# Causal triangle of a score maximum added in 64-row tiles instead of 128-row tiles

## The reference

```python
q = (x @ Wq + bq).reshape(b, t, 16, 8).transpose(0, 2, 1, 3)     # 16 heads of 8
k = ...; v = ...                                                # 4 groups, each repeated for 4 heads
q, k = _rope(q), _rope(k)
scores = jnp.einsum('bhtd,bhsd->bhts', q, k) / sqrt(8)
scores = jnp.where(tril, scores, -inf)
probs = jax.nn.softmax(scores, axis=-1)
attn = jnp.einsum('bhts,bhsd->bhtd', probs, v)
out = attn.transpose(0, 2, 1, 3).reshape(b, t, 128) @ Wo + bo
```

## Time and profile before

| what | us |
|---|---|
| median of 3 runs | 2346.62 (2346.45 to 2359.24) |
| span of the profiled execution | 2345.2 |
| PE busy | 2106.0 (90%) |
| DVE busy | 1792.4 (76%) |
| ACT busy | 1629.6 (69%) |
| POOL busy | 1377.0 (59%) |
| L648 in the causal stage, PE busy: pa, pc, pb | 50.3, 36.7, 31.1 (256, 256 and 192 products) |

### The profile page before, as it was taken

One profiled execution on the slowest core, in us unless ns is written; L12 is line 12 of the kernel. 1 busy time (PEld: TensorE's weight loads), 2 busy tenths in 40 slices (PEclk: granted clock), 3 DMA queues, 4 the chain that ended last, 5 costly groups with the idle time before them and its releaser, 6 DMA issues. The chain is left out here.

```text
span 2345.2 us, 55664 instructions
## 1 busy us (share of the span) xinstructions
PE 2106.0 (90%) x19389; PEld 1356.7 (58%) x19516; DVE 1792.4 (76%) x3455; ACT 1629.6 (69%) x3312; POOL 1377.0 (59%) x2085
## 2 busy tenths in 40 slices
PE   2999999999999368999999999999999999999971
PEld 1555555555555246666666666666666666666641
DVE  2788787787877266888888888886888788787736
ACT  1676576666767346888878878776877787777745
POOL 3587687777876675465564655554564564564403
PEclk8999999999999668999999999999999999999985
DMA  1000001000100101101001010111011001001014
GB/s 35 2 20 24 16 15 29 15 15 15 29 15 10 37 17 47 32 18 33 16 16 32 16 32 16 27 34 31 18 26 26 18 21 31 18 17 34 18 33 112
DMA packets 50491, 59.34 MB, mean 25 GB/s; under 512 B 8144, under 2 KB 43392, under 8 KB 48256
## 3 DMA queue, kind: packets, MB, share of 16 engines
q1 hardware_dynamic: 50304, 56.58, 9.7%
HBM read 17.90 MB, written 8.39 MB: 11 GB/s over the span
## 5 line engine op out<-in xcount | busy, mean ns | idle before, releaser
L974 POOL TENSOR_TENSOR b_part_b<-b_raw,b_tabs 128x256 f32<-128x256 f32 x512 | 431.8, 873 | 326.5 <-ACT b_raw L1033 291.8
L983 POOL TENSOR_TENSOR b_qk<-b_qk,b_part_b 128x1024 f32<-128x1024 f32 x128 | 332.4, 2597 | 282.5 <-DVE b_qk L1133 275.3
L1133 DVE TENSOR_TENSOR b_qk<-b_raw,b_tabs 128x512 f32<-128x512 f32 x256 | 282.2, 1141 | 0.1
L417 POOL TENSOR_TENSOR a_idle<-a_idle 128x1 f32<-128x1 f32 x432 | 83.3, 193 | 232.2 <-ACT a_probs L511 163.4
L1234 PE MATMUL b_work<-b_w_high,b_h_high 128*128 128x512 f32 x384 | 190.6, 496 | 29.6 <-DVE b_h_low L1123 19.0
L468 POOL TENSOR_SCALAR_AFFINE_SELECT a_probs<-a_probs 128x256 f32<-128x256 f32 x512 | 204.5, 411 | 0.0
L579 DVE TENSOR_REDUCE a_qpack<-a_pc 128x2 f32<-128x768 f32 (+1 forms) x128 | 139.4, 1089 | 61.6 <-PE a_pc L648 60.0
L1261 PE MATMUL b_work<-ident,b_qk 128*128 128x128 f32 x1024 | 161.3, 289 | 25.9 <-issue 15.7
L1305 PEld LDWEIGHTS b_work<-b_v_even,b_pT 128*64 128x64 f32 x2048 | 138.5, 139 | 78.4 <-issue 75.8
L679 PE MATMUL a_work<-a_probs,a_v 128*32 128x512 f32 (+3 forms) x2048 | 182.8, 453 | 1.1 <-POOL a_probs L468 0.8
L1060 ACT COPY b_pT<-b_work 128x512 f32<-128x512 f32 x256 | 155.5, 608 | 35.9 <-PE b_work L1295 35.8
(11 more groups left out here) (206 smaller groups left out, 5481.1 us busy)
## 6 DMA issues: line engine op xcount, KB each, us to landing
b_v_even<-b_v SPq DMA_DIRECT2D x32, 528.0 KB, 4.4
b_v_even<-b_v SPq DMA_DIRECT2D x32, 396.0 KB, 5.8
a_x_in<-in_L_attn_x SPq DMA_DIRECT2D x16, 256.0 KB, 3.2
a_x_again<-in_L_attn_x SPq DMA_DIRECT2D x16, 256.0 KB, 3.3
x_scratch<-a_x SPq DMA_DIRECT2D x16, 256.0 KB, 2.4
out<-c_y SPq DMA_DIRECT2D x4, 1024.0 KB, 5.4
b_w_raw<-in_L_ffn_wqkv SPq DMA_DIRECT2D x2, 768.0 KB, 4.4
b_tabs<-tab SPq DMA_DIRECT2D x2, 512.0 KB, 4.1
```

Of the source, the lines that this page charges most:

```text
L974: last = pool.tensor_tensor(part_b[:, x, :].rearrange("p (h d) -> p h d", d=DH)[:, :, lo:lo + DH // 2], raw[:, i % 2, x, :].rearrange("p ( ...
L983: pool.tensor_tensor(qk[:, i], qk[:, i], part_b[:], ALU.add).then_inc(c_made, 1)
L1133: last = dve.tensor_tensor(qk[:, i, x, :].rearrange("p (h d) -> p h d", d=DH), raw[:, i % 2, x, :].rearrange("p (h d) -> p h d", d=DH), ta ...
```

## The change

The triangle is added by four products of 64 rows instead of two of 128. The first two (a = 0 and 1) add it to the queries 0 to 63 of a block over all 128 keys, the other two to the queries 64 to 127 over the keys 64 to 127; nothing is masked for those below. The stationary operand is a slice of `half_of`, ones on a diagonal of a 64 x 192 field, once in each half of the partitions: by its start column (64 or 0) the ones stand in the columns of the first or the second half of the queries. The moving operand is `mask_half`, the triangle for 64 queries, also held twice. The setup makes them with one more memset, and three more selects.

```diff
--- before.py
+++ after.py
@@ -304,7 +304,8 @@
         bo_b = sb("bo", [P, D])
         cos = sb("cos", [P, TT, QK1])
         sin = sb("sin", [P, TT, QK1])
-        mask_ts = sb("mask_ts", [P, P], BF16)
+        mask_half = sb("mask_half", [P, P], BF16)
+        half_of = sb("half_of", [P, P + HALF], BF16)
 
         xn = sb("xn", [P, TT, D])
         xT = sb("xT", [D, T])
@@ -343,7 +344,7 @@
         freed = {name: sem(f"a_{name}_freed") for name in bank_of}
         flow = Banks(PLAN1, bank_of, filled, freed)
 
-        LOADS, CONSTS_MADE = 16, 12
+        LOADS, CONSTS_MADE = 16, 16
         transfers = lambda b, slot: (b - slot) * 8
         halves = lambda a: slice(HALF * a, HALF * a + HALF)
 
@@ -398,14 +399,21 @@
 
         @block.gpsimd
         def _(pool):
-            for t, val in [(ident, 0.0), (ident_bf, 0.0), (mask_ts, 0.0), (qpack, 0.0), (kpack, 0.0), (v, 1.0), (idle, 0.0)]:
+            for t, val in [(ident, 0.0), (ident_bf, 0.0), (mask_half, 0.0), (half_of, 0.0), (qpack, 0.0), (kpack, 0.0), (v, 1.0),
+                           (idle, 0.0)]:
                 pool.memset(t[:], val).then_inc(consts_made, 1)
-            pool.wait_ge(consts_made, 7)
+            pool.wait_ge(consts_made, 8)
             for t in (ident, ident_bf):
                 pool.affine_select(out=t[:], in_=t[:], compare_op=ALU.not_equal, fill=1.0, base=0,
                                    pattern=[[-1, P]], channel_multiplier=1).then_inc(consts_made, 1)
-            pool.affine_select(out=mask_ts[:], in_=mask_ts[:], compare_op=ALU.is_ge, fill=MASKED, base=0,
-                               pattern=[[-1, P]], channel_multiplier=1).then_inc(consts_made, 1)
+            for a in range(2):
+                r = slice(HALF * a, HALF * a + HALF)
+                pool.wait_ge(consts_made, 10 + 2 * a)
+                pool.affine_select(out=mask_half[r, :], in_=mask_half[r, :], compare_op=ALU.is_ge, fill=MASKED, base=0,
+                                   pattern=[[-1, P]], channel_multiplier=1).then_inc(consts_made, 1)
+                pool.affine_select(out=half_of[r, :], in_=half_of[r, :], compare_op=ALU.not_equal, fill=1.0, base=HALF,
+                                   pattern=[[-1, P + HALF]], channel_multiplier=1).then_inc(consts_made, 1)
+            pool.wait_ge(consts_made, 14)
             for e in range(2):
                 pool.memset(packed_k(e, NEG_MAX, 1), 1.0).then_inc(consts_made, 1)
             pool.wait_ge(consts_loaded, 16 * LOADS)
@@ -644,10 +652,13 @@
                         r = halves(a)
                         pe.matmul(x[:, a, n * w:(n + 1) * w], qT[r, slot, j, i * P:(i + 1) * P], kT[r, slot, gp, 0:w],
                                   start=(n == 0), stop=False, skip_group_check=True)
-                for a in range(2):
-                    last = pe.matmul(x[:, a, 0:len(js) * w].rearrange("p (j s) -> p j s", s=w)[:, :, i * P:w], ident_bf[:],
-                                     mask_ts[:].rearrange("p (a c) -> p a c", a=1).to_broadcast([P, len(js), P]),
-                                     start=False, stop=True, skip_group_check=True)
+                for first in (0, HALF):
+                    for a in range(2):
+                        r, n = halves(a), P - first
+                        last = pe.matmul(x[:, a, 0:len(js) * w].rearrange("p (j s) -> p j s", s=w)[:, :, i * P + first:w],
+                                         half_of[r, HALF - first:HALF - first + P],
+                                         mask_half[r, 0:n].rearrange("p (a c) -> p a c", a=1).to_broadcast([HALF, len(js), n]),
+                                         start=False, stop=True, skip_group_check=True)
                 last.then_inc(full, 1)
 
             def max_turn(l, b, j, slot):
```

## The result

The kernel after takes 2329.41 us (2324.02 to 2330.76, 4 runs), the kernel before 2347.36 beside it (2346.45 to 2359.24): a ratio of 0.9908, interval 0.9885 to 0.9931. The forecast was 2326. Its sum was not right in its parts, though: in the profiled execution, which took 2324.02 us, the causal stage gave 31 us where 21 were expected, and the stage behind it, whose code is unchanged, took 7 back.

What follows compares the result with a forecast made beforehand. PE was taken to lead 15 of a causal step's 44 us, DVE and POOL the other 29. 14 x 1.13 + 5 x 0.9 + 0.7 = 21 us off the median 2346.6 gave 2326 us, range 2304 to 2342.

Steps and rivals of the forecast that it cites:

- The prices of the fills: Mask cost per score-bank fill: one head saves 0.14 or 0.27 or loses 0.02, four heads save 0.43; 3.8 us a step.
- loads in front: Rival, chance 0.05: mask products wait for weight loads not fetched ahead behind f32 tiles, 1.6 us a step more, 2370.
- loads eat it: Rival, chance 0.14: each fill's four mask loads are not covered and use up the shape-change savings; 6 us left, 2340.
- issue: Rival, chance 0.03: issuing small products costs 0.054 each, so four masks take 0.22, 0.13 more than priced; 2344.
- PE bounds all: Rival, chance 0.06: PE bounds the whole causal step, so all 3.8 us count in 15 steps, 57 us; 2289.
- The slack is larger than I read: Rival, chance 0.22: DVE and POOL stretches hide waits or some fills move them forward; half the sum counts, 37 us, 2308.
- so PE has 0.11 to spare there: At values 9, behind POOL's apply and selects: PE starts 0.16 after them, a real wait takes 0.05; 0.11 us gained.
- Fills 13 to 10: Score-bank fills 13, 6, 3, 2, 7, 11, 16, 10, in the stretch from values 9 that PE was said to lead.
- the loss at fill 2: Its bank is read until 419.07, so of 0.61 us that PE would be earlier, 0.36 turns into waiting.
- fill 14: One-head masks before a 64*128 group, in the stretch that PE leads: saves 0.27 us.
- 0.12 to spare: DVE's cast starts 0.16 after POOL's rotary chain ends, so PE's earlier finish gains 0.12 us there.
- The steps with a jump: Five causal steps where the hardware loop jumps back and PE stands 2.83 us: more fills count, 0.9 us extra each.

Runs made afterwards that it cites:

- e_shape: The changed kernel with each of its four 64-row mask products over all 128 keys, the tile shape without the saved columns: 2327.72 us, ratio 0.9921 to before.

## Why the forecast came out near, and what failed in it

**The prices of the fills held.** No 0.11 stands in front of the masks, the next 64*128 group pays one load, transposes pay the change of shape. The loads of the four products are hidden. By lines, their group over the causal stage:

```profile
L658 PEld LDWEIGHTS a_pc<-a_mask_half,a_half_of 64*128 64x128 bf16 x512 | 15.0, 96 | 20.0 <-issue 15.2
```

96 ns each, beside 97 for 128 rows and 187 for the f32 ones; since four masks with their loads pass in 0.09 us before a 64*128 group, they cannot lie in front of the products or be bound by issue. That ends three rivals (loads in front, loads eat it, issue). The Trainium skill (TensorE: Matmul & The Clock Gate, "Weight-path perf modes — Fast Weight Load (FWL) and DoubleRow") says that the quick load is on for 128 weights of a type that is not FP32. The two lengths agree with it and halving the rows does not undo it; no run here switches it off for a bf16 load. The Trainium skill (TensorEngine Tiling (Array Packing), "Key Properties") says that a change of tiling mode drains TensorE. The trace fits it: the masks' start came 0.10 nearer to the scores', and e_shape shows that the shape, not the columns, is most of the gain. No run tells a drain from the weight loading that the prediction took those 0.11 us for.

**The rivals on the slack.** "PE bounds all" fell with PE's idle time of 1.34 us. "The slack is larger than I read" came closest for the causal stage: 31 us, between the forecast's 21 and its 37 (which make 2310, not the 2308 that stands beside them).

**The step that failed** is the second of the chain, "so PE has 0.11 to spare there", at *values* 9. *Values* 9 stands behind that select in the list, but the count it waits for belongs to an earlier one, which had ended some 2 us before. What closes the stretch over DVE and POOL is u_turn, 4.3 us earlier (410.85), and its spare was 0.59. The step in three parts, from starts in the rows:

| part of the step | before | after | saved | predicted |
|---|---|---|---|---|
| x_turn to POOL's first rstd (398.12 - 381.64; 384.33 - 368.02) | 16.48 | 16.31 | 0.17 | 0.27 + 0.12 |
| rstd to u_turn (410.85; 396.47) | 12.73 | 12.14 | 0.59 | 0 |
| u_turn to x_turn (425.62; 410.26) | 14.77 | 13.79 | 0.98 | 0.63 + 0.11 |

The second part holds no PE work that counts, only the spare. In the third, PE leads from u_turn and not from *values* 9 on, so fill 1 counts too: 0.40 of the 0.98. Fills 13 to 10, priced at 0.63 with the loss at fill 2, gave 0.58. In the first part fill 14 gave 0.17 and not 0.27. Its 0.12 to spare did arrive: the cast starts 6.06 behind POOL's rotary chain (372.66 to 378.72) instead of 6.19 (430.43 to 436.62), and waits for POOL now. But from the cast's start to the end of the variance DVE takes 3.71 instead of 3.59 and gives it back. The cast lasts 0.75 instead of 0.62 there, which is not the reason. In the change with u_turn moved it also begins behind a wait and lasts 0.43, the variance is the longer for it, and the stretch takes 3.76. The cast and the variance of that run, and the variance of before:

```profile
378.01 0.43 DVE L576 CAST a_qpack<-a_turned 128x512 fp32r<-128x512 f32 x1 [0.18 <-POOL a_turned L452]
...
380.09 1.68 DVE L562 TENSOR_SCALAR a_var<-a_mv 128x4 f32<-128x4 f32 x1
```

```profile
438.89 1.31 DVE L553 TENSOR_SCALAR a_var<-a_mv 128x4 f32<-128x4 f32 x1
```

Most other plain steps of the changed kernel have 3.76 too, and take 42.27 to 42.29 where this one takes 42.24. Why the stretch has these lengths is open; the prediction took it as fixed. So 0.59 + 0.40 + 0.58 + 0.17 = 1.74 of this step, where the prediction had 0.11 + 0.90 + 0.12 = 1.13. The quarter taken off the apply confirms the place: the step follows it by 0.31.

**PE's wait for DVE** was to grow from 0.5 to over 1 us at fill 21's maxima. It is 0.73; the idle time went to three places, 0.30 (POOL's select, *values* 1), 0.73 and 0.24 (u_turn).

**The steps with a jump** were priced at 0.9 more than a plain one and gave 1.0 (2.7 less 1.7). They were taken as fixed in number and place, though, and that was the second fault: no term of the sum stood for the jumps of the unchanged stages. With two more of them stalling, the local stage took 7.4 us longer in the profiled execution; without that it would have been some 2317 (2324.0 - 7.4). That the sum landed within 4 us of the median is luck: two errors of opposite sign, 10 us too little for the causal stage and 7 not taken off for the local one, and on top of them the median lies 5 us above the execution from which these parts are read.

## What to carry to other kernels

Small products in another tile shape than their neighbours cost more by the two changes of shape (0.10 us each here) than by their columns; put them in the neighbours' shape, even if it takes twice as many. Before a gain is priced by the spare at a wait, read from the count which increment the wait is for, and look at every place where the led engine meets the chain, not at the one with the nearest time. And where a program has hardware loops, compare the kernels by plain steps: an edit that adds or moves code can shift the time by more than it is worth itself.

## What the runs showed of the hardware

A jump back in a loop of some 1500 to 1900 PE instructions a turn may cost nothing or, as in the step of 49.92 above, 7.6 us (8.1 in another step of that run), though all turns run the same code. PE stands for 1.9 to 4.5 us with no wait, at some jumps in two pieces, and then goes on at a lower granted clock (0.61 in the window above). In the changed kernel at such a place:

```profile
442.69 0.77 PE L677 MATMUL a_pc<-a_qmT,a_kT 64*128 64x512 f32 x2 [2.23 <-issue]
```

Which jumps stall, in the causal loop, the first and the second local loop, five in each, from the profiled executions:

| kernel | stalls |
|---|---|
| before | 5, 0, 5 |
| change | 5, 2, 5 |
| tile shape alone | 5, 1, 5 |
| change, order of products | 5, 1, 5 |
| change, u_turn moved | 5, 2, 5 |
| change, a quarter off the apply | 5, 2, 5 |
| before, u_turn moved | 0, 1, 5 |
| before, no masks | 0, 5, 5 |
| before, 528 waits between the stages | 5, 1, 5 |
| either, waits in front | 5, 5, 5 |
| loops written out, all three | none |

Each row is one execution, and executions of one kernel differ by up to 15 us (2344.01 to 2359.41 for before), as much as two or three stalls cost, so a count may well change from run to run. The two loops of the local stage are the same code twice, and differ. Neither the loop's size nor its place settles it, since before with u_turn moved has both unchanged. Where a jump stalls, the packets show code fetched again in pieces of about 16 KB all through the turn, and where none stalls, nothing is fetched; what decides between the two is open. What was not foreseen is the size: the same hidden waits moved the time by 29 us in one kernel and by about 13 in the other, and writing the loops out gave 52 and some 60 us, more than the change under study.
